# One prelude for the grouped attention, stacked products in the delta rule, another norm order, and two unread products in each delta step

## The reference

```python
# x: (2, 1024, 256) fp32; each layer is x = x + f(layernorm(x))
at1: 16 heads of 128, causal softmax attention with biases            # L0_attn_a
ff2: silu(x Wg) * (x Wu), rms_norm, down; weights ternary, FF = 1024   # L0_ffn
dr3: delta rule, 16 heads of 16, chunks of MB = 16 tokens              # L0_attn_b
    k = rotary(x Wk.T); v = x Wv.T; W = I
    def step(W, kc, vc):                    # one chunk
        z = kc @ W
        return W - kc.T @ ((z - vc) * 2 / 256), z
    out = layernorm(z) * gamma + beta; return out @ Wo.T
ff4: as ff2
ga5: 32 query heads and 8 key heads of 8, rotary, softmax, no mask     # L1_attn_a
ff6: Hadamard-rotated silu feed-forward, FF = 1024                     # L1_ffn
at7: 16 heads of 128, causal, ALiBi                                    # L1_attn_b
ff8: as ff6
```

## Time and profile before

| | us |
|---|---|
| median of 3 runs (lowest, highest) | 3950.96 (3939.65, 3962.98) |
| the profiled execution, and its span | 3935.7, 3933.8 |
| loads, ln1 and at1 | 0 to 1031 |
| ff2 | 1031 to 1176 |
| dr3: preparation, main block from 1231, loop from 1253.8 | 1176 to 1516 |
| ff4 | 1516 to 1660 |
| ga5: preparation to 1779.7 | 1660 to 2547 |
| hw6 | 2547 to 2586 |
| ff6 | 2586 to 2745 |
| at7 | 2745 to 3768 |
| ff8 | 3768 to 3933.8 |

### The profile page before, as it was taken

How to read it: one execution, slowest core, us unless ns; L and a number is a source line. 1 busy time by engine, 2 the same in 40 slices (tenths; PEclk the granted TensorE clock), 3 DMA queues, 4 the chain that set the end, 5 groups by cost and what they waited for, 6 DMA issues and landing times. The chain is left out here.

```text
span 3933.8 us, 54900 instructions
## 1 busy us (share of the span) xinstructions
PE 3584.9 (91%) x20008; PEld 2589.1 (66%) x20020; DVE 2498.3 (64%) x4874; ACT 1941.6 (49%) x4114; POOL 840.2 (21%) x826
## 2 busy tenths in 40 slices
PE   6999999999889997848999999789899999999989
PEld 5777877778666895623333333358777777777767
DVE  5666666656554665528888888344566666666643
ACT  3555555555442323304777777522455555555532
POOL 1111011100132452322000000020344443444410
PEclk9999999999889998867999999989999999999999
DMA  1000000000000000022111110010000000000000
GB/s 50 17 10 18 10 18 15 12 9 2 22 1 2 1 0 21 1 107 58 31 30 31 44 31 17 37 43 1 22 11 12 8 11 5 11 8 9 2 38 17
DMA packets 38792, 78.13 MB, mean 20 GB/s; under 512 B 7056, under 2 KB 17168, under 8 KB 35984
## 3 DMA queue, kind: packets, MB, share of 16 engines
q1 hardware_dynamic: 38544, 74.82, 6.4%
HBM read 56.97 MB, written 15.73 MB: 18 GB/s over the span
## 5 line engine op out<-in xcount | busy, mean ns | idle before, releaser
L1610 DVE TENSOR_REDUCE ga5m_nm<-ga5m_M 128x1 f32<-128x1024 f32 x512 | 604.4, 1218 | 85.6 <-PE ga5m_M L1514 82.4
L1599 ACT ACTIVATE ga5m_pr<-ga5m_E 128x512 f32<-128x512 f32 x1024 | 539.5, 603 | 209.8 <-PE ga5m_E L1550 206.3
L432 PE MATMUL at_A<-at_pT,at_V 128*128 128x512 f32 (+3 forms) x1536 | 519.8, 488 | 12.0 <-issue 5.0
L353 POOL TENSOR_TENSOR at_prob<-at_prob,at_slope_row 128x128 f32<-128x128 f32 (+7 forms) x256 | 369.7, 1447 | 577.4 <-DVE at_prob L650 577.3
L432 PEld LDWEIGHTS at_A<-at_pT,at_V 128*128 128x128 f32 x1536 | 283.9, 190 | 254.6 <-issue 204.3
L520 ACT ACTIVATE at_pT<-at_T 128x512 f32<-128x512 f32 (+3 forms) x768 | 347.1, 488 | 102.0 <-PE at_T L473 100.7
L1514 PE MATMUL ga5m_M<-ga5m_K,ga5m_Q 64*128 64x512 f32 x1024 | 304.0, 465 | 73.0 <-DMA ga5m_Q<-ga5m_zero 55.6
L1550 PEld LDWEIGHTS ga5m_E<-ga5m_Q,ga5m_K 64*128 64x128 f32 x1024 | 162.4, 185 | 313.1 <-ACT ga5m_pr L1599 304.8
L1550 PE MATMUL ga5m_E<-ga5m_Q,ga5m_K 64*128 64x512 f32 x1024 | 363.6, 447 | 3.9 <-ACT ga5m_pr L1599 3.6
L473 PE MATMUL at_T<-all_ident,at_prob 128*128 128x128 f32 x2304 | 336.4, 273 | 7.8 <-ACT at_pT L520 7.4
L473 PEld LDWEIGHTS at_T<-all_ident,at_prob 128*128 128x128 f32 x2304 | 268.3, 140 | 30.4 <-issue 7.7
(11 more groups left out here) (298 smaller groups left out, 8524.6 us busy)
## 6 DMA issues: line engine op xcount, KB each, us to landing
ga5m_Q<-ga_qs SPq DMA_DIRECT2D x64, 256.0 KB
at_raw_qk<-in_pqk SPq DMA_DIRECT2D x32, 256.0 KB, 2.9
ga_qs<-ga5s_part SPq DMA_DIRECT2D x8, 1024.0 KB
at_raw_v<-in_pv SPq DMA_DIRECT2D x16, 256.0 KB, 3.3
at_raw_o<-in_po SPq DMA_DIRECT2D x32, 128.0 KB, 2.0
ga5m_K<-ga_ks SPq DMA_DIRECT2D x32, 128.0 KB
all_X<-in_x SPq DMA_DIRECT2D x1, 2048.0 KB, 7.4
at_raw_t<-in_gu SPq DMA_DIRECT2D x8, 256.0 KB, 3.5
```

The lines of the kernel that those rows point to most:

```text
L353: nc.gpsimd.tensor_tensor(dst[:, 0:end], dst[:, 0:end], slope_row[n // 2 % 2][:, 0:end], ALU.add).then_inc(ramp_done, 1)
L432: mm = nc.tensor.matmul(bank[:, lo:GQ * P], V[b][:, kt, col:col + DH], pT[g][:, kt, lo:GQ * P], start=(kt == 0), stop=(kt == GQ * (g + 1) ...
L1599: nc.scalar.activation(pr[e % NR][:, :], Eb[e % 3][:, :], ACT.Exp, scale=scale).then_inc(e_done, 1)
L1610: nc.vector.tensor_reduce(nm[half % 2][:, m:m + 1], Mb[v % 2][:, :], AX.X, ALU.max, negate=True).then_inc(m_free[v % 2], 1)
```

## The change

First attention: the two comparisons leave `take` and stand at steps MEAN + 2 and MEAN + 3, one at each; ROUND moves from 7 and 9 to 8 and 11. Feed-forward: `turn` at f = 5 for 4; both `low_turned` at f = 6; measuring of the next layer's norm for group g - 2 at f = 0, its normalising of the last but one group at f = 6 of the last group, and the last group in halves. Hadamard weights: the lows of the first eight pieces on VectorE, of the last four on GpSimd. Grouped attention: one block for rotary products, values, splitting, storing (48 stores of up to 128 rows of 512 columns) and the loads of units 0 to 2, which SP issues behind item 8; K, Q and `zero` are allocated outside it; Q is filled whole. Delta rule: one block that makes k and v tile by tile and stores k|v, high and low, in DRAM (kvs); then in each tile stacks KS (high, high, low of the keys) and KVS (high, low, high of k|v) of 48 rows, chunk by chunk, are loaded by three DMAs of 16 partitions each, KS by ScalarE's queue, KVS by SP's; the product is fp32r, with 48 of 128 rows filled, and the masks and MK are gone. In each step j of 1 to 7 of each tile two fp32 products of 256 columns go into the bank of Z that the step doesn't use; nobody reads them. Before the loop stand four such products of 512 columns and one of 256 for each of the 16 pairs.

```diff
...
-            ROUND = [(4 * (i // 2) + 2) * QT + (7, 9)[i % 2] for i in range(len(pieces))]
+            ROUND = [(4 * (i // 2) + 2) * QT + (8, 11)[i % 2] for i in range(len(pieces))]
+
+            CUT = {MEAN[i] + 2 + x: (i, x) for i in range(len(pieces)) for x in range(2)}
...
+                if t in CUT:
+                    cut(*CUT[t])
...
-                    if f == 4 and g + 1 < NG:
+                    if f == 5 and g + 1 < NG:
                         turn(g + 1)
...
+                if f == 0 and nxt is not None and g >= 2:
+                    next_measure(g - 2, range(2, GT))
+                    next_shifted(g - 2, range(GT))
...
-                    if g:
+                    if g == NG - 1:
                         next_measure(g - 1, range(2, GT))
-                        next_shifted(g - 1)
-                if f in (6, 7) and g + 1 < NG:
-                    low_turned(g + 1, f - 6)
+                        next_shifted(g - 1, range(GT))
+                if f == 6:
+                    if g + 1 < NG:
+                        low_turned(g + 1, 0)
+                        low_turned(g + 1, 1)
+                    elif nxt is not None:
+                        next_normalise(g - 1, range(GT))
             low(NF - 1)
-            if nxt is not None:
-                next_normalise(NG - 2, range(GT))
...
+                if 0 < k <= n1:
+                    low(k - 1)
...
+            order = ([("r", i) for i in range(2 * NJ)] + [("v", t) for t in range(NT // 2)]
+                     + [("r", i) for i in range(2 * NJ, 4 * NJ)] + [("v", t) for t in range(NT // 2, NT)])
+
+            @block.sync
+            def _(sp):
+                for i, (n, k) in enumerate(work):
+                    M = jobs[k][2]
+                    cols = slice(n * N, (n + 1) * N)
+                    for x, done in enumerate((high_done, low_done)):
+                        sp.wait_ge(done, i + 1)
+                        for twice in range(2):
+                            dst = qs[k * 16:(k + 1) * 16, x, twice, :, cols] if k < 2 else ks[:, twice, x, :, cols]
+                            sp.dma_start(dst, part[i % NPART][0:M, x, :].bitcast(F32)
+                                         ).then_inc(stored[i % NPART], 16)
+                    if i == 3 * NJ - 1:
+                        sp.wait_ge(fill_done, 2 + 5 * NSLOT)
+                        for x in range(NPART):
+                            sp.wait_ge(stored[x], 64)
+                        for unit in range(NSLOT):
+                            load(sp, unit)
...
+        def load_keys(engine, t, b):
+            for part, first in ((0, 0), (0, C), (1, 2 * C)):
+                engine.dma_start(KS[b][first:first + C, :, :].bitcast(F32),
+                                 kvs[part, rows_of(t, b), 0:D].rearrange("(j s) n -> s j n", s=C)
+                                 ).then_inc(k_in[b], 16)
+
+        def load_both(engine, t, b):
+            for part, first in ((0, 0), (1, C), (0, 2 * C)):
+                engine.dma_start(KVS[b][first:first + C, :, :, :, :].rearrange("p j v c n -> p j (v c n)").bitcast(F32),
+                                 kvs[part, rows_of(t, b), :].rearrange("(j s) n -> s j n", s=C)
+                                 ).then_inc(kv_in[b], 16)
...
+                    if i in (7, 9):
+                        b = (i - 7) // 2
+                        sp.wait_ge(zero_done, 2 * BATCH)
+                        wait_stored(sp, 0, b)
+                        load_keys(sp, 0, b)
+                        load_both(sp, 0, b)
...
+                for t in range(1, QT):
+                    for b in range(BATCH):
+                        sp.wait_ge(pp_done, (t - 1) * NP + (b + 1) * DC * PC)
+                        load_both(sp, t, b)
...
+                for t in range(QT):
+                    for b in range(BATCH if t + 1 < QT else 0):
+                        act.wait_ge(pp_done, t * NP + (b + 1) * DC * PC)
+                        load_keys(act, t + 1, b)
+                    if t:
+                        copy_z(t - 1, (t - 1) % 2)
...
                     for e in range(2):
-                        mm = nc.tensor.matmul(PP[p % 2][:, e, :, :], MK[q % 2][:, 2 * pair + e, :],
-                                              KV[:, bass.ds(t + b * QT, 1), c, :, :].rearrange("p a v n -> p (a v n)"),
-                                              start=True, stop=True)
+                        mm = nc.tensor.matmul(PP[p % 2][:, e, :, :], KS[b][:, 2 * pair + e, c * P:(c + 1) * P],
+                                              KVS[b][:, 2 * pair + e, :, c, :], start=True, stop=True)
...
+                        if j:
+                            if j == 1:
+                                pe.wait_ge(z_out, t + 2)
+                            for x in range(2):
+                                nc.tensor.matmul(Z[1 - slot][:, 2 * x:2 * x + 2, :].rearrange("p q n -> p (q n)"),
+                                                 consts["ident"][:, :], hm[:, :, :].rearrange("p v n -> p (v n)"),
+                                                 start=True, stop=True)
+
+                def busy(width):
+                    nc.tensor.matmul(Z[1][:, :, :].rearrange("p q n -> p (q n)")[:, 0:width], consts["ident"][:, :],
+                                     kT[:, 0, 0:width], start=True, stop=True)
...
+                for i in range(4):
+                    busy(512)
                 for p in range(NP):
                     product(0, p)
+                    busy(256)
...
```

More of the change, by code:

```diff
@@ new lines, in grouped_attention @@
+        o.ctx.callback(o.clear)
+        NSLOT = 3
+        Q = [o.sb(f"Q{i}", [P, NQ * SEQ], F32R) for i in range(NSLOT)]
+        K = [o.sb(f"K{i}", [P, SEQ], F32R) for i in range(NSLOT)]
+        zero = o.sb("zero", [2, P])
+        q_in = [o.sem(f"q_in{i}") for i in range(NSLOT)]
+        NPART = 6
+        N = 512
+        spare = [t[:, :, :].rearrange("p c n -> p (c n)") for t in room]
+        part = [spare[i // 4][:, i % 4 * 2 * N:(i % 4 + 1) * 2 * N].rearrange("p (k n) -> p k n", n=N)
+                for i in range(NPART)]
@@ L1478, in maxima @@
                                          mpart[h % 2][:, k, :].bitcast(F32)).then_inc(ms_in[h % 2], 16)
[L1480 to L1483 removed]
+                for i in range(NPART):
+                    sp.wait_ge(stored[i], 128)
                 for h in range(NH):
@@ L1666, in delta_rule, with rows_of @@
-        turn(nc, name + "k", kT, lambda c, g: KV[:, 4 * g:4 * g + 4, c, 0, :], consts, False)
+        KS = [o.sb(f"KS{b}", [P, NC, D], F32R) for b in range(BATCH)]
+        KVS = [o.sb(f"KVS{b}", [P, NC, 2, DC, P], F32R) for b in range(BATCH)]
+        k_in = [o.sem(f"k_in{b}") for b in range(BATCH)]
+        kv_in = [o.sem(f"kv_in{b}") for b in range(BATCH)]
+        stored = [o.sem(f"stored{i}") for i in range(NK)]
+        def rows_of(t, b):
+            return slice((b * QT + t) * P, (b * QT + t + 1) * P)
@@ new lines, in wait_stored @@
+        def wait_stored(engine, t, b):
+            i = order.index(b * QT + t)
+            engine.wait_ge(stored[i % NK], 32 * (i // NK + 1))
+        def load_keys(engine, t, b):
[8 more added lines that the diff above has]
+                                 ).then_inc(kv_in[b], 16)
```

469 lines of the change are left out of this document (308 added, 161 removed).

## The result

The changed kernel takes 3827.13 us (median of 4 runs, 3826.55 to 3842.94), the kernel before 3945.31 in the same runs: a ratio of 0.9708, with an interval of 0.9659 to 0.9756. The forecast was 3832 with a range of 3800 to 3868. It was counted from a median of 3951 over three runs; in the rounds of the experiments the kernel before has medians of 3938.6, 3942.6 and 3940.2 (7 to 9 runs each), so against 3827 the change is worth 112 to 118 us by the medians.

A forecast was written before the change was run, and what follows sets the result against it. TensorE, busy 91% of the span, was taken as the bound, with gains at its waits and cheaper products. Terms -58 - 15 - 34.5 - 12 + 0.5 = -119 took the median from 3951 to 3832 us, range 3800 to 3868.

The forecast's parts named there:

- Grouped attention, -58: Grouped attention before its main loop: first rotary to first score product falls from 119.0 to 60.5 us.
- my bounds of -62 to -45: Grouped attention's preparation: -62 with issues at their shortest, -45 if loads and stores crowd each other for 13 us.
- The step on the loads: Grouped attention's preparation: loads issued about 42.5 us in, 24 issues taking 12.9, 12 stores 5.2, SP ending at 60.5.
- Rival 2: Transfers bind both preludes and the loop: delta rule gains nothing, grouped attention 45; 3885 us, chance 0.08.
- Norm order, -34.5: Four feed-forward stages: shorter waits at group boundaries; ff8 -9, ff6 -9.5, ff2 and ff4 -8 each.
- The step that failed: Feed-forward: slow product groups after the boundary waits go too, -2.4 a Hadamard stage; none counted in the ternary stages.
- Rival 1: Feed-forward stages' waits only change their name: 17 us gained instead of 34.5, 3850 us, chance 0.14.
- First attention, -12: First attention: moving the cuts later removes most of TensorE's waits for the addition to X, -12 us.
- the far bound: First attention: the largest gain allowed, -15.6 us, in a range of -4 to -15.6.
- The Hadamard lows: Hadamard weights: eight subtractions move from GpSimd to VectorE, last four pieces 0.5 late; +0.5 us (-1 to +1).
- Delta rule, -15: Delta rule: +8 before the loop, -2 at its start, +4 for a wait in the first tile, -25 loop.
- The row that I rested on: Delta rule's loop: full clock (2.4 GHz) over 45 us in the last tile, so nothing suggests less with more columns.

The follow-up runs named there:

- e5_unit_values: Changed kernel with only unit 0 loaded in the grouped attention's preparation and all 16 value tiles after the 12 rotary items: 3807.29 us.
- e3_one_unit: Changed kernel with only unit 0 loaded in the grouped attention's preparation, units 1 and 2 in the main block: 3812.63 us.
- the second: Profile from running the changed kernel again without any edit: median 3834.98 us, the profiled execution at 3824.7.
- e7_old_cut: Changed kernel with the first attention's two comparisons back behind the scale and the rounding at steps 7 and 9: 3858.56 us.
- e8_old_delta: Changed kernel with the whole function delta_rule of the kernel before: 3829.94 us.
- e1_no_idle: Changed kernel without the two unread products in each delta rule step, warm-up products before the loop kept: 3917.45 us.
- e9_idle_two_tiles: Changed kernel with the unread products in the first two tiles of the delta rule alone: 3879.08 us.
- e12_half_width: Combination kernel (one unit, values last, one unread product, none in last tile) with that product 128 columns wide, not 256: 3803.90 us against 3782.64.

## Why the prediction was right, and where it wasn't

The sum was -119 against a profile, and -111 came; against the medians, 3832 and 3827. The terms were less good than the sum: two errors of 17 and 11 us have opposite signs. That the sum came out so near is therefore in part luck, and so is the median: the three runs of the kernel before that it was counted from lay some 10 us above the later ones (3951 for 3939 to 3943), which offset the 8 us that the change fell short.

*Grouped attention, -58, measured -41.2*, outside my bounds of -62 to -45. The rows of SP's queue in the first profile (start, time in the queue, what):

```profile
1659.78 0.35 SPq L1386 DMA_DIRECT2D ga_K<-ga_ks  x1
...
1675.61 7.51 SPq L1425 DMA_DIRECT2D ga_qs<-tern_w  x8
1683.17 2.77 SPq L1425 DMA_DIRECT2D ga_ks<-tern_w  x4
```

The block begins at 1608.8. The step on the loads failed three times. They are issued 51.0 us in and not 42.5: I put all value tiles at the end, where the diff has eight of them ahead of items 6 to 8, and left the fills out of the way to item 8 (e5_unit_values: 5.5, and 3 that are argued). The 24 issues take 15.8 us and not 12.9. And the 12 stores, taken at 0.43 each, take 10.3 us, 0.86 each. Two parts make these 5.1 us. The first is the price itself: 0.43 was taken from no row of such a store. In a quiet queue, with the DMA engines at 0.10, two of them take 1.23 us:

```profile
1618.08 1.23 SPq L1425 DMA_DIRECT2D ga_qs<-tern_w  x2
```

At 0.64 from one to the next, twelve are 7.7 us, 2.5 over the forecast. The other 2.6 lie in a few long issues among ordinary ones, most of it in the first, 1.75 us above the 0.60 of the others:

```profile
1675.61 2.35 SPq L1425 DMA_DIRECT2D ga_qs<-tern_w  x1
```

So the queue's state doesn't make each store dearer. Among the loads too one issue, at 1671.14, takes 2.54 us and holds most of their 2.9. Busy DMA engines alone don't do it either. In the delta rule's preparation the stores are issued while these engines are as full (1.10), and ten of them take 0.43 to 0.50 each; only the last two, behind 16 issues without a pause, take 1.94 and 1.76:

```profile
1193.24 0.43 SPq L1831 DMA_DIRECT2D dr_kv<-dr3p_kvh  x1
```

```profile
1193.00:1198.00 5.00, 2.06 (x12) 1.54 (x10) 2.24 (x4) 1.72 (x3) 0.00 (x0) 1.00 1.10 275
```

What makes a single issue long is not shown; in each of these places it stands late in a long run of issues.

8.5 + 2.9 + 5.1 and 0.8 for the change of block are the 17.4 us (the prediction's parts add up to 60.6 and not 60.5). The mechanism, SP's queue as the end of the block, was right; e3_one_unit takes it away and gets 13.2 of them back. Rival 2 had this gain at 45.

*Norm order, -34.5, measured -45.4.* The mechanism and the waits came as forecast where they were worked out: 0.4 us in the Hadamard stages, 1.4 to 1.7 in the ternary ones, where I had said about 2. The step that failed is the clock: I counted the slow product groups behind the waits for the Hadamard stages (-2.4) and left them out for the ternary ones, whose waits are longer. There they are worth 7.4 us in ff2 by the first profile, half of its gain, and 4.9 by the second. ff2 and ff4 hold 7.7 of the 10.9 us that were missed, and ff6 4.4, where the products are busy for 3 to 4 us less (2.4 had been counted); no run splits ff6 further. ff8 came 1.2 short. Rival 1, that the waits change their name, came true in a small part: the waits for hf and for hT1l rose by 3.5 and 3.2 us over the four stages.

*First attention, -12, measured -14.4*, near the far bound: the wait for all_X is gone, not only shortened, as e7_old_cut shows. The Hadamard lows came at +0.4 for +0.5.

*Delta rule, -15, measured -11.8, and of that 6 to 8 by the change.* Its terms hit, but for the loop: preparation +9.4 to the end of the wait for hm for +8, the products before the loop 17.8 us for 18.3, a wait of 4.0 for 4, a step of 3.13 for 3.13, and at a tile's end a wait of 0.5 for 0.8. The loop, from its first product to the first behind it, takes 201.6 us for 220.3, -18.7; with the wait of 4 in it -21 had been forecast. The stacks' loads (GB/s in 40 slices of 1250:1280):

```profile
GB/s 0 0 158 223 101 113 135 134 109 115 115 160 101 108 23 0 0 0 27 270 113 111 112 154 112 102 107 131 150 105 78 33 0 0 0 137 214 112 112 122
```

Most slices of their plateau have 100 to 115 GB/s, some up to 160; I took 113. The Trainium skill, page "SBUF — State Buffer", section "Door 1: The DMA port swizzle", gives 109 for 16 neighbouring partitions; most slices of the trace agree. Missed was what follows the wait of 4 us: TensorE's clock is 0.74 from 1237 to 1250, some 3 us. That e8_old_delta finds 5.4 us of the stage's difference in code that is the same shows a limit of the method: two executions of the same code differ by some us in a stage, and one profile of each kernel can't tell that from the change.

*What I didn't ask.* I priced the two unread products at 0.86 us a step, 48 us in all, and took the clock as given "with more columns in the step". With them in place both were right. But the text gives no reason why they stand there, and its price for them has the wrong sign: without them the loop takes 79 us more (e1_no_idle). The row that I rested on, full clock in the last tile, is of a loop of pairs alone, back to back; it says nothing on pairs with fp32r products between them.

## What to carry to other kernels

When fp32 products are replaced by faster fp32r ones, look at the granted clock before counting the gain; a busy TensorE can sit at half clock, and products that nobody reads can then be worth more than they cost, but one at a time is tried, since the second here only cost. A wait at a stage's boundary is priced with the products behind it, which may run at half clock, and not alone. A DMA issue is priced from a row of the same transfer (0.60 us for the grouped attention's stores, 0.43 for the delta rule's, both in rows with no long issue), with room for single issues of 2 us and more behind a long burst; and loads that the next block doesn't need at once belong behind its start. Before a change of clock is put down to the work in a step, look for the last wait ahead of it.

## What the hardware did that I had not expected

With two unread fp32 products of 256 columns in a step, and with one, the granted clock is 1.00 in the delta rule's loop once it has come back from the wait for the first stack (at 1250 in the changed kernel); with one of 128 columns it moves between 0.50 and 1.00; with none it is 0.50 from that wait on, at a busy share of 97%, and doesn't come back in 270 us. Where it falls from 1.00 within the loop, a wait at a tile's end stands just ahead of it: 1.33 us in e9_idle_two_tiles, 1.11 in e12_half_width, where three waits of the same length before it had no such effect. Waits of 0.98 us and less there never did, in the kernel before neither. Whether the wait or the work in the step decides is open: one more unread product at the tile's end alone, to cover the wait, was not tried. Why the same pairs hold full clock in the last tile, where they stand alone, is not shown by these runs either.

The end of the grouped attention's loop runs at 1.00 in some executions and at 0.50 in others of the same kernel, which is 16 us of 3830 and splits the runs of the changed kernel into two groups. Which of them comes differs between kernels whose code there is the same. The cause stays open; no run here tried unread products in that stretch.
